# Graph network kernel: registers for sixteen steps in one load, adjacency columns fetched during the build, and two small edits around them

## The chip, the cores and the metric

The kernel runs on 1 core of one Trainium2 chip. The metric is the device time in microseconds (us) from launch to end, as the median of several executions. Engines: TensorE (PE; its weight loads are PEld, its sequencer PEq or PEldq), VectorE (DVE), ScalarE (ACT), GpSimd (POOL) and SyncE (SP), which here only issues DMAs.

## What is computed

Four graph layers over 3125 nodes with 128 features and 53125 directed edges (self loops included, sorted by destination), each added to x. The change lies in what comes before and in the first of them:

```python
h = jnp.maximum(_layernorm(x, axis=-1), 0.0)
x = x + _L0_gnn_ref(h, L0_gnn_W, L0_gnn_b, L0_gnn_gamma, L0_gnn_beta, edge_index)
# _L0_gnn_ref(x, W, b, gamma, beta, edge_index):
xw = x @ W
deg = jax.ops.segment_sum(ones, dst, num_segments=N)          # dst with N further self loops
dinv = jnp.where(deg > 0, jax.lax.rsqrt(deg), 0.0)
msg = xw[src] * (dinv[src] * dinv[dst])[:, None]
h = jax.ops.segment_sum(msg, dst, num_segments=N) + b
h = (h - mean) * jax.lax.rsqrt(var + BN_EPS) * gamma + beta   # mean, var over the nodes
h = x + jax.nn.relu(h)
```

Three more layers follow (a graph convolution with attention, a gated network of five rounds, an attention layer). They read the same edge counts and are not touched.

## The kernel before

All layers work on a dense matrix of edge counts, `adj`, 128 x 196 windows x 400 half-precision numbers in the chip's main memory. A window is 16 destination nodes; in it stand the counts of all sources. It is built once.

**The build** (`adjacency_counts`, span 37 to 335 us). The sorted edges are cut into 416 tiles of 128, and a tile that crosses a window's border is used again for the next, which gives `BSTEPS` = 611 steps. In each step DVE makes a one-hot `hot` of 400 columns (line 886; a ring of `HRING` = 8), every eighth step a one-hot `low` for eight steps (line 876), and PE adds `low`ᵀ `hot` to the PSUM bank of the step's window (line 958). Which bank that is, and how many banks must have been freed before, is data: both stand in `route_r`, two integers a step, and PE's sequencer loads them into registers:

```python
if j % 4 == 0:
    e.load(regs, route[0:1, 2 * j:2 * j + 8])
```

In the profile this is a TENSOR_LOAD of line 923, and the preparation of the eight values is one FUSED_REGOPS of line 924. A window is full after about three steps. Then ACT copies its bank to `stage` (line 975), which is a ring of `SRING` = 8, clears the bank of the window before (line 978), and SP stores the stage to `adj` (line 987). `WR` = 4 banks take turns. ACT reads the step at which each window is full from `until_r`, in loads of `WL` = 4 registers (line 970). DVE may be 8 steps ahead of PE, since a slot of the ring is free when the matmul that read it is done (`made`).

**Other work in the same loop**, at steps given by tables: node degrees on DVE (`degree_at`, steps 100 to 320, lines 842 and 846), twenty products of weights for a later layer (`fold_at`, every 12th step from 40 to 268, PE at line 938, DVE copies at line 900), and the first layer's own xw scaled by dinv, `own`, in seven groups of up to four node tiles (`hw_at`, every 16th step from 342, lines 952, 954, 909, 912). GpSimd gathers `near`, normalizes x to `h` (lines 813, 816) and casts each group of `own` to `parts[:, :, 0, :]` (line 827). The loop ends with the stores' landing and a barrier of all engines.

**The first layer** (`gcn_first`, from 335 us). The product own x adj goes by 8 chunks of destination columns (1, 3, 3, 3, 3, 4, 4 and 4 tiles of 128). SP loads a chunk to `cols` (two buffers, line 1025), DVE adds the nodes' own edges on the diagonal (`add_own`, line 1051, one operation a tile) and widens the half-precision counts to `stream` in five pieces (`widen`, line 1061), and PE multiplies (line 1138, 50 matmuls a chunk; each tile of `own` in two parts, the rounded one and the rest, which DVE makes at line 1073, `far`). Ahead of the third chunk's load stand on SP's queue eleven small loads of vectors and of the next layer's weights. PE's product for chunk 0 cannot begin before the chunk has landed, its own edges are in and a piece is widened.

## Time and profile before

| | |
|---|---|
| runs | 3403.79 us median of 3 (3402.35 to 3407.19) |
| profiled execution, its own time | 3405.62 us |
| profiled execution, span from first to last instruction | 3403.8 us, granted clock 0.861 |
| build loop | 37 to 335 us of the span |
| product of the first layer on PE | 340.3 to 421.2 us |
| busy over the whole span | PE 82%, weight loads 63%, DVE 52%, ACT 40%, POOL 28% |

The busy shares are means over stages with different limits, and the change touches only the span from 37 to about 421 us. So the rows further down are all from there, but for one from a later stage that has the same kind of instruction.

### The profile page before, as it was taken

Reading aid. Unit: us, or ns where it says so; the run is one execution under the profiler, and the core shown is the slowest. Engines: PE = TensorE matmul, PEld = TensorE weight load, DVE = VectorE, ACT = ScalarE, POOL = GpSimd, SP = SyncE. Lnnn points to the kernel's source line nnn. Section 1 sums busy time; section 2 is a strip of 40 time slices with the busy share of each in tenths; the row PEclk is TensorE's granted clock in tenths of the full one; section 3 lists DMA queues with packets and bytes.
Section 4 is the critical chain, followed back from the end, with each engine's and each line's share of the span. In section 5 each row is a group of like instructions: output and inputs, shape, how many; then the busy total and the mean of one; then the engine's idle time right before and its main releaser. Section 6 shows DMA issues by size and latency. Waiting matters only on the chain. (4 is left out here: it accounts for less than half of the span.)

```text
span 3403.8 us, 41036 instructions
## 1 busy us (share of the span) xinstructions
PE 2807.8 (82%) x13998; PEld 2155.1 (63%) x13998; DVE 1760.0 (52%) x4016; ACT 1368.7 (40%) x2596; POOL 961.7 (28%) x779
## 2 busy tenths in 40 slices
PE   5776977899998699999999999999844445446998
PEld 3333875577776578787877787877533334445775
DVE  7987765999977452111122112111534543356994
ACT  3565034699997221111111112111323333342896
POOL 6100043000000453232322231321177777750000
PEclk9977979899999799999999999999855555555999
DMA  4232633101100432121212121310242221113100
GB/s 135 100 101 88 263 130 155 39 40 40 44 1 1 192 150 97 58 92 68 87 63 90 65 92 57 116 70 1 74 141 47 46 46 38 29 21 126 78 35 20
DMA packets 79695, 266.66 MB, mean 78 GB/s; under 512 B 21129, under 2 KB 53344, under 8 KB 70176
## 3 DMA queue, kind: packets, MB, share of 16 engines
q1 hardware_dynamic: 62520, 236.50, 18.6%
q0 software_dynamic: 16976, 27.54, 3.7%
q8 instruction: 121, 1.98, 0.2%
q14 instruction: 78, 0.64, 0.1%
HBM read 232.80 MB, written 31.18 MB: 78 GB/s over the span
## 5 line engine op out<-in xcount | busy, mean ns | idle before, releaser
L2799 PE MATMUL psum<-gate_stream,parts 128*128 128x384 f32 (+1 forms) x3600 | 667.9, 344 | 16.9 <-POOL gate_stream L2872 12.5
L2799 PEld LDWEIGHTS psum<-gate_stream,parts 128*128 128x128 f32 x3600 | 631.5, 189 | 33.8 <-issue 14.4
L2872 POOL CAST gate_stream<-gate_adj 128x1920 fp32r<-128x1920 f16 (+1 forms) x200 | 371.1, 1863 | 851.3 <-PE psum L2799 828.2
L2153 PE MATMUL psum<-gat_h,gat_pair 128*128 128x129 f32 (+1 forms) x3750 | 571.1, 291 | 8.6 <-DVE gat_pair L1957 7.7
L2153 PEld LDWEIGHTS psum<-gat_h,gat_pair 128*128 128x128 f32 (+1 forms) x3750 | 461.5, 191 | 123.4 <-issue 77.7
L1485 POOL DMA_INDIRECT edge_rows<-edge_table,src_idx x440 | 431.7, 981 | 180.7 <-issue 133.7
L2890 DVE SCALAR_TENSOR_TENSOR gate_work<-psum,bhh,gate_work 128x384 f32<-128x384 f32 (+1 forms) x80 | 50.0, 626 | 793.7 <-PE psum L2762 763.1
L1957 DVE SCALAR_TENSOR_TENSOR gat_pair<-gat_above,gat_adj 128x512 f32<-128x512 f32 (+3 forms) x525 | 326.6, 622 | 86.8 <-PE psum L2153 56.7
L2066 ACT ACTIVATE gat_above<-psum,gat_as 128x512 f32<-128x512 f32 (+3 forms) x525 | 329.7, 628 | 41.4 <-PE psum L2141 39.9
L2057 ACT ACTIVATE psum<-gat_ad_rows,gat_as 128x512 f32<-128x512 f32 (+3 forms) x525 | 334.9, 638 | 16.9
L1912 DVE SCALAR_TENSOR_TENSOR gat_acc<-gat_adj,gat_q,gat_acc 128x512 f32<-128x512 f16 (+3 forms) x497 | 328.4, 677 | 0.0
L2816 ACT COPY x<-psum 128x384 f32<-128x384 f32 (+1 forms) x72 | 31.9, 488 | 545.5 <-PE psum L2799 545.5
L1722 PE MATMUL psum<-edge_rows,edge_hot 128*128 128x81 f32 x826 | 179.6, 419 | 86.0 <-DVE edge_rows L1621 86.0
L1722 PEld LDWEIGHTS psum<-edge_rows,edge_hot 128*128 128x128 f32 x826 | 177.2, 332 | 87.6 <-issue 87.2
L958 PE MATMUL psum<-count_hot,count_low 128*128 128x400 f16 x611 | 172.9, 412 | 69.8 <-DVE count_hot L886 47.2
L2141 PE MATMUL psum<-gat_r_rows,gat_pick 6*128 6x512 bf16 (+7 forms) x525 | 189.1, 361 | 0.9 <-ACT gat_r_rows L2075 0.9
L958 PEld LDWEIGHTS psum<-count_hot,count_low 128*128 128x128 f16 x611 | 88.6, 146 | 155.1 <-issue 122.3
L886 DVE TENSOR_SCALAR count_hot<-iota_hot,keyt 128x400 f16<-128x400 f16 x611 | 175.5, 339 | 16.3 <-PE psum L958 13.3
L2844 ACT ACTIVATE gate_work<-psum,brz 128x384 f32<-128x384 f32 (+1 forms) x80 | 47.1, 588 | 331.7 <-PE psum L2775 331.7
L2383 POOL MEMSET parts<- 128x512 f32 x1 | 0.5, 526 | 547.3 <-POOLq L2283 547.3
L975 ACT CAST count_stage<-psum 128x400 f16<-128x400 f32 x196 | 96.8, 494 | 126.2 <-PE psum L958 124.6
L1649 ACT ACTIVATE edge_hot<-iota,edge_minus 128x128 f32<-128x128 f32 x413 | 121.3, 391 | 6.2 <-PEq L2458 6.2
(486 smaller groups left out, 3700.8 us busy)
## 6 DMA issues: line engine op xcount, KB each, us to landing
gate_adj<-adj SPq DMA_DIRECT2D x35, 2400.0 KB, 8.1
gat_adj<-adj SPq DMA_DIRECT2D x8, 3200.0 KB, 11.3
adj<-count_stage SPq DMA_DIRECT2D x196, 100.0 KB, 1.6
gcn_adj<-adj SPq DMA_DIRECT2D x8, 2400.0 KB, 8.2
edge_place<-row_scratch SPq DMA_DIRECT2D x40, 352.0 KB, 3.8
gate_adj<-adj SPq DMA_DIRECT2D x5, 2800.0 KB, 9.1
gcn_adj<-adj SPq DMA_DIRECT2D x4, 3200.0 KB, 10.0
edge_rows<-edge_table,src_idx POOLq DMA_INDIRECT x440
```

What stands on the lines that cost most here:

```text
L886: e.tensor_scalar(hot[:, j % HRING, :], iota_hot[:], keyt[:, j:j + 1], None, ALU.is_equal).then_inc(hots, 1)
L958: e.matmul(flat[:, bass.ds(at[j % 4], ROW)], low[:, j // LS % LRING, :, j % LS], hot[:, j % HRING, :], start=False, stop=False, skip_group ...
L1485: e.indirect_dma_start(out=rows[:, c % 2, s, 0:ROWS], out_offset=None, in_=table, in_offset=bass.IndirectOffsetOnAxis(ap=self.src_idx[:, k ...
L1722: mm = e.matmul(flat[:, bass.ds(to[k % 4], SUMS)], hot_of(c)[:, s, :], rows[:, c % 2, s, :], start=False, stop=False, skip_group_check=True)
L1912: e.scalar_tensor_tensor(on, of, q[:, hi, h:h + 1], on, ALU.min, ALU.max).then_inc(most, 1)
L1957: e.scalar_tensor_tensor(on(pair, g % 2), on(above, g % 3), 1e30, cols[:, u % ring, 0:width(u) // W, hi * W:(hi + 1) * W], ALU.min, ALU.mu ...
L2057: e.activation(ps[:, 4 + g % 3, 0:up - lo], ad_rows[:, h, lo:up], ACT.Relu, bias=as8[:, hi, h:h + 1], scale=1.0 - NEG).then_inc(relus, 1)
L2066: e.activation(above[:, g % 3, 0:width(u)], ps[:, 4 + g % 3, 0:width(u)], ACT.Exp, bias=as2[:, hi, h:h + 1]).then_inc(exps, 1)
L2141: e.matmul(ps[:, 4 + g % 3, 0:width(u)], pick[:, h, :], r2_rows[:, u % 2, 0:width(u)], start=False, stop=False, skip_group_check=True).the ...
L2153: mm = e.matmul(ps[0:p, b, a:a + D + 1], pair[:, g % 2, i * P:i * P + p], h1[:, hi, h, :], start=hi == 0 and i % 3 == 0, stop=hi == NT - 1 ...
L2799: mm = e.matmul(ps[:, f, 0:hi - lo], parts[:, t, m, f, :], stream[:, (NGG * i + t // GG) % GR, 0:windows(i), t % GG * W:(t % GG + 1) * W], ...
L2872: e.tensor_copy(stream[:, n % GR, 0:windows(i), :], cols[:, i % 2, 0:windows(i), g * GW:(g + 1) * GW]).then_inc(widened, 1)
```

## The change

Five edits:

1. PE's registers are loaded for `RL` = 16 steps at once (32 registers) in place of 4 steps (8 registers): 39 loads in place of 153. `route_r` and `lowt` are padded to a multiple of 16.
2. ACT's registers are loaded for 14 windows at once in place of 4: 14 loads in place of 49.
3. The columns of chunks 0 and 1 are loaded inside the build, when windows 16 and 40 have been stored (SP waits there for the stores of the windows that the chunk reads), and not behind the barrier.
4. The own edges of these two chunks are added by DVE in the last four steps of the build (`own_at`), each behind a wait for the load. `ident_h` is made at the build's start.
5. The second part of `own` (`far`) is made by GpSimd inside the build, right behind its cast.

To make room for `cols` in the build, several temporaries of the stage before and of the build now lie in tiles that are used only later (`wl` in `own`, `near` in `parts`, `hot_f`, `key_f`, `low_f` and `low_i` in `folded`, `node_row` in `h`, `later` in `norms`); their instructions are the same.

```diff
-WL = 4
+WL = 14
+RL = 16
...
-        wl = self.sb("wl", [P, LAYERS, 2, S2], F32, st)
+        wl = own[:, 0:4 * LAYERS, :].rearrange("p (l j a) w -> p l j (a w)", l=LAYERS, j=2)
...
-                    e.tensor_copy(parts[:, at, 0, :], own[:, at, :])
+                    e.tensor_copy(parts[:, at, 0, :], own[:, at, :]).then_inc(rounded, 1)
+                    e.wait_ge(rounded, n // 2 + 1)
+                    e.tensor_tensor(parts[:, at, 1, :], own[:, at, :], parts[:, at, 0, :], ALU.subtract)
...
+        own_at = {BSTEPS - 1: (0, 0), BSTEPS - 2: (1, 0), BSTEPS - 3: (1, 1), BSTEPS - 4: (1, 2)}
...
+                    if j in own_at:
+                        c, i = own_at[j]
+                        t, p = tiles[c][i]
+                        e.wait_ge(loaded[c], 16)
+                        on = cols[:, c, 8 * i:8 * i + p // W, t * W:(t + 1) * W]
+                        e.tensor_tensor(on, on, ident_h[:, 0:p].rearrange("p (w n) -> p w n", n=W), ALU.add)
...
-                regs = [e.alloc_register(self.name("route_reg")) for _ in range(8)]
+                regs = [e.alloc_register(self.name("route_reg")) for _ in range(2 * RL)]
...
-                    if j % 4 == 0:
-                        e.load(regs, route[0:1, 2 * j:2 * j + 8])
+                    if j % RL == 0:
+                        e.load(regs, route[0:1, 2 * j:2 * (j + RL)])
...
-                    e.wait_ge(freed, need[j % 4])
+                    e.wait_ge(freed, need[j % RL])
...
+                    for c, (lo, hi) in enumerate(spans[:2]):
+                        if w == hi // W + SRING:
+                            for s in range(SRING):
+                                e.wait_ge(stored[s], 16 * (hi // W // SRING))
+                            e.dma_start(cols[:, c, 0:(hi - lo) // W, :], self.adj[:, lo // W:hi // W, :]).then_inc(loaded[c], 16)
...
-                e.tensor_copy(ident_h[:], self.ident[:]).then_inc(seen, 1)
-                for n in range(NT // grp):
-                    at = slice(n * grp, (n + 1) * grp)
-                    e.tensor_tensor(parts[:, at, 1, :], own[:, at, :], parts[:, at, 0, :], ALU.subtract).then_inc(far, 1)
-                    if n == 0:
-                        e.wait_ge(seen, 1)
-                        add_own(0)
-                        for g in range(GS):
-                            widen(0, g)
-                widen(0, GS)
-                add_own(1)
+                for g in range(NGG):
+                    widen(0, g)
```

PE, the build's step 48, before: the load of registers (line 923), its preparation, a product of the folds (line 938), then the step itself; the ISA row of line 958 carries the step's wait.

```order
L923 TENSOR_LOAD route_r
L924 ISA
L938 MATMUL psum<-wih,wl 128x384 x2
L958 ISA
L958 MATMUL psum<-count_hot,count_low 128x400
```

The same place of the changed kernel, where one load in four is left:

```order
L935 TENSOR_LOAD route_r
L936 ISA x2
L937 ISA x2
L950 MATMUL psum<-wih,own 128x384 x2
L970 ISA
L970 MATMUL psum<-count_hot,count_low 128x400
```

The load stands there once in 16 steps and not once in 4, it fills 32 registers, and four instructions prepare them in place of one. The other rows are the same (`own` is now where `wl` lies).

DVE, from the last step of the build to the first pieces of chunk 1, before:

```order
L886 TENSOR_SCALAR count_hot<-iota_hot,keyt 128x400 [waits counts_made] x6
L805 UNCONDITIONAL_BRANCH
L1044 UNCONDITIONAL_BRANCH [waits barrier_Pool_Activation_PE_DVE_SP_release]
L1070 CAST gcn_ident<-ident 128x128
L1073 TENSOR_TENSOR gcn_parts<-own,gcn_parts 128x5x128
L1051 TENSOR_TENSOR gcn_adj<-gcn_adj,gcn_ident 128x8x16 [waits first_loaded0,first_seen]
L1061 CAST gcn_stream<-gcn_adj 128x640 [waits first_own_in]
L1061 CAST gcn_stream<-gcn_adj 128x640 x3
L1073 TENSOR_TENSOR gcn_parts<-own,gcn_parts 128x5x128 x4
L1061 CAST gcn_stream<-gcn_adj 128x640 [waits first_streamed]
L1051 TENSOR_TENSOR gcn_adj<-gcn_adj,gcn_ident 128x8x16 [waits first_loaded1]
L1051 TENSOR_TENSOR gcn_adj<-gcn_adj,gcn_ident 128x8x16 x2
```

The same stretch of the changed kernel, whose widening is line 1075:

```order
L905 TENSOR_TENSOR gcn_adj<-gcn_adj,gcn_ident 128x8x16 [waits first_loaded1]
L892 TENSOR_SCALAR count_hot<-iota_hot,keyt 128x400 [waits counts_made]
L905 TENSOR_TENSOR gcn_adj<-gcn_adj,gcn_ident 128x8x16 [waits first_loaded0]
L808 UNCONDITIONAL_BRANCH
L1058 UNCONDITIONAL_BRANCH [waits barrier_Pool_Activation_PE_DVE_SP_release]
L1075 CAST gcn_stream<-gcn_adj 128x640 x4
L1075 CAST gcn_stream<-gcn_adj 128x640 [waits first_streamed]
L1086 TENSOR_TENSOR x<-x,h_23 128x3200
L1075 CAST gcn_stream<-gcn_adj 128x1920 [waits first_streamed] x4
```

The wait for a load moved from behind the barrier to ahead of it, four additions of own edges with it, and the five subtractions are gone from DVE.

SP, the stores of the build and what comes between them in the changed kernel:

```order
L999 DMA adj<-count_stage 128x400 [waits counts_evicted] x17
L1004 DMA gcn_adj<-adj 128x3200 [waits counts_stored4,counts_stored5,counts_stored3,counts_stored6,counts_stored2,counts_stored7,counts_stored1,counts_stored0]
L999 DMA adj<-count_stage 128x400 [waits counts_evicted] x24
L1004 DMA gcn_adj<-adj 128x9600 [waits counts_stored4,counts_stored5,counts_stored3,counts_stored6,counts_stored2,counts_stored7,counts_stored1,counts_stored0]
L999 DMA adj<-count_stage 128x400 [waits counts_evicted] x155
```

Before, the 196 stores stood in one row there, and both loads came first behind the barrier.

## Rows read from the trace of the kernel before

**Rows 1.** Windows: length, then busy us (count) of PE, PEld, DVE, ACT, POOL; clock, DMA.

```profile
84.00:150.00 66.00, 45.63 (x159) 24.50 (x158) 64.16 (x155) 32.85 (x76) 12.04 (x6) 0.90 0.27 96
150.00:332.00 182.00, 132.77 (x495) 71.36 (x494) 143.98 (x474) 110.14 (x251) 6.47 (x11) 0.84 0.27 90
```

**Rows 2.** PE's weight loads in time: start, us, engine, operation, idle before.

```profile
49.28 0.81 PEld L958 LDWEIGHTS psum<-count_hot,count_low 128*128 128x128 f16 x4 [0.94 <-issue]
...
326.07 0.85 PEld L958 LDWEIGHTS psum<-count_hot,count_low 128*128 128x128 f16 x4 [0.89 <-issue]
```

**Rows 3.** Register loads and their preparation, by line: ns min/median/max, first and last start.

```profile
L923 PEldq TENSOR_LOAD <-route_r x153: 587/592/1162, 37.0 to 328.6; - x153
L924 PEldq FUSED_REGOPS  x153: 80/150/158, 37.8 to 329.3; - x153
L1720 PEldq TENSOR_LOAD <-edge_out_r x117: 328/333/338, 2574.0 to 3074.3; - x117
L970 ACTq TENSOR_LOAD <-until_r x49: 304/308/576, 37.0 to 325.9; - x49
```

**Rows 4.** Matmuls of the build in order of time, around a fold.

```profile
54.81 1.55 PE L958 MATMUL psum<-count_hot,count_low 128*128 128x400 f16 x4 [0.45 <-ACT psum L978]
56.35 2.92 PE L938 MATMUL psum<-wih,wl 128*128 128x384 f32 x4
59.06 3.21 PE L958 MATMUL psum<-count_hot,count_low 128*128 128x400 f16 x12
```

**Rows 5.** Groups of the build, 37 to 332 us: PE's folds, DVE's one-hots.

```profile
L938 PE MATMUL psum<-wih,wl 128*128 128x384 f32 x80 | 34.5, 558 | 10.2 <-issue 10.2
...
L886 DVE TENSOR_SCALAR count_hot<-iota_hot,keyt 128x400 f16<-128x400 f16 x611 | 175.5, 339 | 16.3 <-PE psum L958 13.3
L876 DVE TENSOR_TENSOR count_low<-iota_low,lowt 128x1024 f16<-128x1024 f16 x77 | 52.9, 686 | 27.3 <-PE psum L958 26.9
```

**Rows 6.** ACT and DVE in order of time, where DVE does not wait.

```profile
46.42 0.49 ACT L975 CAST count_stage<-psum 128x400 f16<-128x400 f32 x1 [0.78 <-PE psum L958]
46.81 0.50 ACT L978 CAST psum<-count_none 128x400 f32<-128x400 f16 x1
...
292.40 0.68 DVE L876 TENSOR_TENSOR count_low<-iota_low,lowt 128x1024 f16<-128x1024 f16 x1
293.00 1.01 DVE L886 TENSOR_SCALAR count_hot<-iota_hot,keyt 128x400 f16<-128x400 f16 x4
```

**Rows 7.** Operations of GpSimd in the build, and DVE's one-hots beside them.

```profile
86.01 8.42 POOL L816 TENSOR_SCALAR h<-h 128x3200 f32<-128x3200 f32 x1
...
218.36 0.64 POOL L827 CAST gcn_parts<-own 128x512 fp32r<-128x512 f32 x1 [10.78 <-DVE own L912]
...
L886 DVE TENSOR_SCALAR count_hot<-iota_hot,keyt x611: 302/318/8357, 37.4 to 327.3; 128x400 f16<-128x400 f16 x153
```

**Rows 8.** The first layer's start on DVE and SP, in order of time.

```profile
335.03 0.80 SPq L1025 DMA_DIRECT2D gcn_adj<-adj  x2
...
339.39 0.23 DVE L1051 TENSOR_TENSOR gcn_adj<-gcn_adj,gcn_ident 128x128 f16<-128x128 f16 x1 [3.36 <-DMA gcn_adj<-adj]
339.65 1.70 DVE L1061 CAST gcn_stream<-gcn_adj 128x640 fp32r<-128x640 f16 x4
...
342.65 0.48 SPq L2231 DMA_DIRECT2D gat_bias<-L_gnn_gat_b  x1
...
344.72 47.86 SPq L1025 DMA_DIRECT2D gcn_adj<-adj  x6
...
345.46 3.49 DVE L1081 TENSOR_TENSOR x<-x,h 128x3200 f32<-128x3200 f32 x1
...
359.00 0.50 DVE L1051 TENSOR_TENSOR gcn_adj<-gcn_adj,gcn_ident 128x128 f16<-128x128 f16 x3 [3.47 <-DMA gcn_adj<-adj]
```

**Rows 9.** PE alone in order of time, 340 to 425 us.

```profile
340.29 80.90 PE L1138 MATMUL psum<-gcn_stream,gcn_parts 128*128 128x128 f32 x400 [9.26 <-DVE gcn_stream L1061]
```

**Rows 10.** Window of PE's product for chunk 0.

```profile
340.00:345.00 5.00, 4.71 (x22) 4.74 (x23) 4.69 (x9) 0.00 (x0) 0.00 (x0) 0.50 0.91 370
```

More of the change, by code:

```diff
@@ L66 @@
 LS = 8
-LP = -(-BSTEPS // LS) * LS
+RL = 16
+LP = -(-BSTEPS // RL) * RL
 LRING = 3
@@ L536, in edge_places, with adjacency @@
         self.rows_last = far("rows_last", [8, STEPS])
-    def adjacency(self, h, own, parts, norms):
+    def adjacency(self, h, own, parts, norms, cols, ident_h, loaded):
         nc = self.nc
@@ L750, in _ @@
                     for g in range(2):
-                        mm = e.matmul(ps[:, 7, t:t + 1], later[:, g, t * P:(t + 1) * P], one_bf[0:ER, :], start=g == 0, stop=g == 1)
+                        mm = e.matmul(ps[:, 7, t:t + 1], later[0:ER, g, t * P:(t + 1) * P], one_bf[0:ER, :], start=g == 0, stop=g == 1)
                 mm.then_inc(tiled, 1)
@@ L792, in adjacency_counts @@
         by_feature = self.sb("first_t", [P, 4 * P], F32, st)
-        shaped, hw_made, hw_taken, norm_kept, norm_in = (nc.alloc_semaphore("first_" + n) for n in (
-            "shaped", "made", "taken", "norm_kept", "norm_in"))
+        shaped, hw_made, hw_taken, rounded, norm_kept, norm_in = (nc.alloc_semaphore("first_" + n) for n in (
+            "shaped", "made", "taken", "rounded", "norm_kept", "norm_in"))
         group = lambda n: range(n // 2 * 4, min(NT, n // 2 * 4 + 4))
@@ L956, in _ @@
                     e.wait_ge(hots, j + 1)
-                    e.wait_ge(freed, need[j % 4])
-                    e.matmul(flat[:, bass.ds(at[j % 4], ROW)], low[:, j // LS % LRING, :, j % LS], hot[:, j % HRING, :],
+                    e.wait_ge(freed, need[j % RL])
+                    e.matmul(flat[:, bass.ds(at[j % RL], ROW)], low[:, j // LS % LRING, :, j % LS], hot[:, j % HRING, :],
                              start=False, stop=False, skip_group_check=True).then_inc(made, 1)
@@ L995, in gcn_spans, with gcn_first @@
         return spans, [[(t, min(P, hi - t * P)) for t in range(lo // P, -(-hi // P))] for lo, hi in spans]
-    def gcn_first(self, own, parts, norms, x1, stats, load, cols, stream, ahead):
+    def gcn_first(self, own, parts, norms, x1, stats, load, cols, stream, ident_h, loaded, ahead):
         nc = self.nc
@@ L1132, in _ @@
                     for t in range(NT):
-                        if c == 0 and t % grp == 0:
-                            e.wait_ge(far, t // grp + 1)
                         if t % GG == 0:
@@ L2218, in gcn_layers @@
         norms = self.sb("norms", [P, NP], F32, first)
-        self.adjacency(h, own, parts, norms)
+        ident_h = self.sb("gcn_ident", [P, P], F16, first)
         cols = self.far("gcn_adj", [P, 2, GC // W, ROW], F16, inner)
+        loaded = [self.nc.alloc_semaphore(f"first_loaded{s}") for s in range(2)]
+        self.adjacency(h, own, parts, norms, cols, ident_h, loaded)
         stream = self.far("gcn_stream", [P, GS, GC // W, GW], F32R, inner)
@@ L2232, in load @@
             return 8
-        self.gcn_first(own, parts, norms, h, stats, load, cols, stream, ahead)
+        self.gcn_first(own, parts, norms, h, stats, load, cols, stream, ident_h, loaded, ahead)
         first.close()
```

57 lines of the change are left out of this document (28 added, 29 removed).

## Prediction

> **What bounds the kernel now.** I read the windows of the build first, then the waits of its engines, then the weight loads, the register loads and the start of the first layer. DVE is nearly full only in one stretch, 84 to 150 us: 64.16 of 66 us [rows 1]. These are the steps 100 to 220 (counted by their register loads), where the degrees run on DVE and one operation of GpSimd, 8.42 us long, holds a one-hot up for 8.36 us [rows 7]. From 150 to 332 us DVE is busy for 144 of 182. No compute engine fills that stretch; PE's sequencer does. Its weight loads come four at a time: 0.81 us of loads, then 0.94 us without any, put down to "issue" [rows 2], so a period of 1.75 us for 4 steps. In the gap stands the load of eight registers, 592 ns, and its preparation, 150 ns [rows 3]; 0.2 us are left for dispatch and the first wait. At the low clock (1.2 GHz at 326 us) the period is 0.85 + 0.89, the same [rows 2], though four matmuls then take 1.55 us [rows 4]. The clock does not set the pace, the sequencer does. "PE waits for DVE count_hot" or "for ACT psum" on a matmul row [rows 4] is mostly this load, since the engine named was done long before. DVE's own idle time, all for PE, is 16.3 + 27.3 = 43.6 us [rows 5].
>
> Behind the build, SP's first load behind the barrier is issued at 335.03, the columns let DVE go on at 339.39 after 3.36 us of waiting [rows 8], and PE starts at 340.29 and then does not stop for 80.9 us [rows 9]. Any us by which it starts earlier is gained if nothing starves it later.
>
> **Edit 1, registers for 16 steps.** The trace has loads of two sizes on this sequencer: 4 registers 333 ns (line 1720), 8 registers 592 ns (line 923) [rows 3]. That is 65 ns a register and 74 ns fixed. By this line, 32 registers take 2.15 us. Preparation is four instructions of 8 values at 150 ns, 0.6 us, and the 0.2 us of dispatch, with three instructions more, I estimate at 0.38. The gap becomes about 3.1 us. Sixteen steps without it take 15 pitches of (0.81 − 0.14)/3 = 0.22 us and a last load of 0.14, 3.5 us. Period for 16 steps: 6.6 us in place of 4 × 1.75 = 7.0. Over 611/16 = 38.2 groups: **−15 us**, if the sequencer paced everything before and after. What goes off:
> - Steps 100 to 220 were paced by DVE, so their fifth brings nothing: +3.
> - One idle stretch of 3.1 us in place of four short ones. DVE can fill its ring of 8 in it (8 × 0.23 + 0.60, about 2.5 us [rows 6]), then waits; sixteen steps of its own take 4.9 us, so at the bare steps it keeps up. Where it has copies or subtractions too, it falls short. A fold takes PE's array for 34.5/20 = 1.7 us [rows 5]. Before, the sequencer ran on meanwhile: the loads went under it, and twelve matmuls then followed without a stop [rows 4]. With 16 steps in one row the fold is hidden only if it does not stand right behind the load, as every fourth does (step 48 and every 48th after). There all ring slots are full and the steps wait for the array: some 1.3 us each, five of them, two in the stretch already left out: +4. Below, this could be nothing; above, 20 × 1.7 = 34 us, if no fold hid at all, but the loads still follow two in three of them closely.
> - The clock: more rest and denser bursts may grant 1.2 GHz more often. Sixteen matmuls then take 16 × 1.55/4 = 6.2 us at most, under the 6.6 us of the sequencer, so I take 0.
>
> Sum for edit 1: **−8 us**.
>
> **Edit 2, ACT's registers.** Loads of 4 take 308 ns [rows 3]; at 65 ns a register, 14 take 0.96 us. ACT stops for about 1.3 us 14 times in place of 0.5 us 49 times. It has slack on the mean, but PE's bursts are now dense. An eviction and a clear take 0.78 us of ACT (twice 0.39 between starts) [rows 6], and a window takes PE 3.1 × 0.22 = 0.68 us in a burst. With four banks PE can go about six steps, 1.4 us, ahead of an open eviction. So a stop of 1.3 us costs from 0 to 0.6 us: 14 × 0.15 = **+2**, between 0 and +8.
>
> **Edit 5, subtraction on GpSimd.** No row has GpSimd with two inputs of 128x512. A cast of that size takes 0.64 us, the clear of 128x3200 8.42 us, so 1.35 for 512 [rows 7]; I take the larger, since two inputs are read. The clear held a one-hot for all of its length, so I count a full stop of DVE: seven times 1.35 us, most of it covered where DVE is up to 8 steps ahead: **+2**, from 0 to 7 × 1.35 = 9. If it took longer than 8 steps of cover, PE would wait for count_hot.
>
> **Edit 3, early columns.** SP's waits for windows 0 to 7 and 0 to 31, behind stores 16 and 40, are for stores long landed. Behind SP's wait stand only further stores. The 2.4 MB move in about 9 us among stores whose ring holds 8 windows, some 12 us at 295/196 = 1.5 us a window: 0, at worst 3 us once. **0**
>
> **Edits 3 to 5 behind the barrier.** DVE's first operation there becomes the widening of chunk 0, at 335.1 in place of 339.65 [rows 8], so PE starts at about 335.7 instead of 340.3: **−4.6**. Is it kept? Chunk 0 takes PE 10.7 us (50 matmuls at the low clock's 4.71/22 = 0.214 [rows 10]), to 346.4. DVE widens five pieces to 337.4, adds x for 3.49 us [rows 8] to 340.9, and has chunk 1 ready. The third chunk's load was issued at 344.72 and arrived at 359.00, 14.3 us later, behind 3.2 MB and eleven small loads [rows 8]. Now the small ones go first, from 335.03 (they ended at 343.1 behind 0.8 us of the two big ones [rows 8]), and it is issued at about 342.4 with no big load ahead: there by 353, and needed when chunk 1's 50 matmuls are done, at about 356. Four own-edge additions of 0.22 us in the build's last steps lie under the last register load: 0. If the landing stayed at 14.3 us, it would come at 356.7 and PE would lose about 2 of the 4.6.
>
> **Sum.** Build −8 + 2 + 2 = −4, behind it −4.6: −8.6 (−9 rounded). The profiled execution took 3405.62 us with a span of 3403.8, so 3396.6 for its like; it lies 1.8 above the median of 3403.79, so the forecast is **3395 us**.
>
> **Rivals.**
> A, the forecast: linear loads, small losses of the bursts. Own range 3386 to 3402, chance 0.50.
> B, the load's time is mostly fixed: then 32 registers take about as long as 8. DVE becomes the bound, and of its 43.6 us of idle time [rows 5] nearly all goes: 3404 − 44 − 5 = 3355. Against it are the 333 and 592 ns, which grow with the number [rows 3]. Chance 0.10. The Trainium skill, "DMA: Bandwidth & Descriptors", section "Latency and other measured facts", gives tensor_load a floor of about 600 ns that unrolling amortizes; read as a cost that stays, it leads to this same time, and a load of 333 ns in this trace lies below such a floor.
> C, the bursts eat edit 1: period of 16 steps stays at 7.0 through folds, ring and ACT; only the 4.6 remain: 3399. The stretch already bound by DVE speaks for it. Chance 0.25.
> D, slower: ACT paces the bursts. A burst of 16 steps closes 5.1 windows, 5.1 × 0.78 = 4.0 us instead of 3.5, and if ACT's long stops cannot be hidden, 14 × 1.3 = 18 us more. Build: +38 × 0.5 + 18 − 8 = +29, with the 4.6 about 3428. It decides as soon as PE waits for a cleared bank more than some 0.9 us a burst in all. Against it: four banks, and ACT idle for 105 of the 248 us of the two windows [rows 1]. A partial case lies at 3412. Chance 0.15.
>
> **Numbers.** A measurement of this kernel tells about 0.2%, 7 us, from no change: 3397 to 3410.6 is the same. Faster: 0.38 of A, all of B, 0.07 of C, 0.55. The same: 0.12 of A, 0.17 of C, 0.03 of D, 0.32. Slower: 0.12 of D and 0.01 of C, 0.13. The range is 3376 to 3411: it leaves out B and most of D, 0.2. A alone is 3386 to 3402.
>
> **What would show it.** Line 935: 39 loads with a median near 2.15 us, two preparations each on lines 936 and 937 of 150 ns. PE's gap every 16 steps near 3.1 us. Build's end at about 331 and not 335, PE's product (line 1141 of the changed kernel) beginning some 9 us earlier, at 331 to 332, with no stop later. One-hots stretched to over 1 us seven times between 218 and 306 us. The prediction is wrong if the load of 32 registers is far from 2.15 us either way, if PE's matmuls wait for ACT's clear in the middle of a burst, or if the build loses more than 4 us to the folds in steps 40 to 268.

## The result: slower by 0.94%

| | before | after |
|---|---|---|
| median, us | 3403.79 (3402.35 to 3407.19) | 3437.51 (3430.25 to 3441.9) |
| ratio | | 1.0094, interval 1.0079 to 1.011 |
| profiled execution, us (its span) | 3405.62 (3403.8) | 3430.25 (3428.6) |
| PE's sequencer, first register load to the last matmul of the build, us | 37.0 to 330.5 | 36.6 to 370.6 |

The forecast was 3395 us, in 3376 to 3411. The kernel is 34 us slower. PE's first product behind the build starts 34.2 us later than in the trace of before, so the whole loss has happened by then; of what follows, some us are given back in the stage of gathers of the profiled execution (32.3 us late at 2377 us of the trace of before, 24.8 at its end).

The same instructions as in [rows 3], in the changed kernel. Columns: engine queue, operation, count, shortest/median/longest ns, first and last start.

```profile
L935 PEldq TENSOR_LOAD <-route_r x39: 2127/2381/2802, 36.6 to 367.3; - x39
...
L936 PEldq FUSED_REGOPS  x77: 80/180/188, 39.0 to 369.7; - x77
...
L937 PEldq FUSED_REGOPS  x77: 42/80/175, 39.5 to 369.9; - x77
...
L982 ACTq TENSOR_LOAD <-until_r x14: 1223/2316/3579, 36.6 to 351.4; - x14
```

PE's load is close to the predicted 2.15 us. ACT's load, predicted at 0.96, has a median of 2.32. Starts and durations alternate: windows 0, 28, 56, ... take 1.2 to 1.5 us and windows 14, 42, ... 3.1 to 3.6.

What PE waits for in the whole build, before and after (line waited for: us in total, times, longest):

```profile
PE psum L958 <- DVE count_hot L886: 47.2, 70, 7.0
PE psum L958 <- ACT psum L978: 20.5, 28, 0.9
PE psum L938 <- issue: 10.2, 19, 0.7
...
PE psum L958 <- issue: 1.6, 4, 0.5
```

```profile
PE psum L970 <- issue: 48.6, 19, 3.5
PE psum L970 <- DVE count_hot L892: 36.6, 18, 5.6
PE psum L950 <- issue: 14.8, 5, 3.1
PE psum L970 <- ACT psum L990: 13.2, 7, 3.3
```

and what DVE waits for after, in the build and then in the steps 112 to 224. There it waited for PE 2.7 us in all before (1.4 and 1.3) and was busy for 52 of 54.6 us.

```profile
DVE count_hot L892 <- PE psum L970: 70.9, 46, 4.4
DVE count_low L881 <- PE psum L970: 4.6, 6, 2.1
```
```profile
DVE count_hot L892 <- PE psum L970: 10.1, 8, 2.1
DVE count_low L881 <- PE psum L970: 3.3, 4, 2.1
```

DVE waited for PE 40.2 us before (13.3 + 26.9 [rows 5]) and 75.5 now, and PE does not stand less for it: 79.5 us before and 113.2 now. Each of the two stands while the other works. The windows of the steps 224 to 608, before and after (length, busy us of PE, PEld, DVE, ACT, POOL, granted clock, DMA share, GB/s):

```profile
153.00:330.00 177.00, 129.23 (x484) 69.59 (x482) 142.06 (x465) 108.26 (x247) 6.47 (x11) 0.84 0.27 90
```
```profile
172.00:370.00 198.00, 126.39 (x480) 76.47 (x479) 146.12 (x463) 105.91 (x247) 14.94 (x18) 0.79 0.25 81
```

The same work takes 21 us longer. PE's weight loads are busy for 6.9 us more, DVE for 4.1 and GpSimd for 8.5 (the subtractions), which does not make 21, and the granted clock is lower.

What a burst costs shows in PE's weight loads around one group of 16 steps (columns as in [rows 2]):

```profile
198.30 0.85 PEld L970 LDWEIGHTS psum<-count_hot,count_low 128*128 128x128 f16 x4 [3.56 <-issue]
199.32 0.17 PEld L970 LDWEIGHTS psum<-count_hot,count_low 128*128 128x128 f16 x1 [0.17 <-issue]
...
201.65 0.70 PEld L970 LDWEIGHTS psum<-count_hot,count_low 128*128 128x128 f16 x4 [0.17 <-issue]
202.69 0.14 PEld L970 LDWEIGHTS psum<-count_hot,count_low 128*128 128x128 f16 x1 [0.33 <-issue]
206.39 0.85 PEld L970 LDWEIGHTS psum<-count_hot,count_low 128*128 128x128 f16 x4 [3.57 <-issue]
```

Four steps go at a pitch of 0.23 us, then seven at 0.33 (six rows are left out). The granted clock of 199.3 to 201.6 us is 0.50, that is 1.2 GHz, and 0.33 us is the pitch of the matmuls there. The gap for the load is 3.56 us instead of 3.1, the period 8.1 instead of 6.6. Behind the build, the barrier is as predicted:

```profile
370.62 0.94 ACT L987 CAST count_stage<-psum 128x400 f16<-128x400 f32 x2 [2.59 <-PE psum L970]
...
373.90 1.70 DVE L1075 CAST gcn_stream<-gcn_adj 128x640 fp32r<-128x640 f16 x4 [5.91 <-PEq L808]
...
374.45 5.81 PE L1141 MATMUL psum<-gcn_stream,gcn_parts 128*128 128x128 f32 x26 [3.42 <-DVE gcn_stream L1075]
```

PE follows DVE's first widening at 0.55 us, where before SP's load at 335.03 stood 5.3 us ahead of PE's start at 340.29 [rows 8, 9]. From the end of the build's last matmul to the product it is 3.4 us and was 9.3. That is why a build 40.5 us longer brings the product only 34.2 us later.

### The profile page after: what moved, and what is told of

Read it like the earlier page. It is cut to its first block and busy times, and to the rows that moved or that the text cites. A ratio compares the mean times of both kernels' runs of the same rounds, so it can differ in the third digit from the quotient of the medians.

```text
span 3428.6 us, 40875 instructions
## 1 busy us (share of the span) xinstructions
PE 2806.3 (82%) x13998; PEld 2160.9 (63%) x13998; DVE 1762.4 (51%) x4011; ACT 1366.1 (40%) x2596; POOL 963.5 (28%) x786
## 5 line engine op out<-in xcount | busy, mean ns | idle before, releaser
L2804 PE MATMUL psum<-gate_stream,parts 128*128 128x384 f32 (+1 forms) x3600 | 667.2, 344 | 15.5 <-POOL gate_stream L2877 11.1
L2804 PEld LDWEIGHTS psum<-gate_stream,parts 128*128 128x128 f32 x3600 | 630.8, 188 | 32.4 <-issue 12.9
L2877 POOL CAST gate_stream<-gate_adj 128x1920 fp32r<-128x1920 f16 (+1 forms) x200 | 370.6, 1861 | 849.9 <-PE psum L2804 828.2
L2060 ACT ACTIVATE psum<-gat_ad_rows,gat_as 128x512 f32<-128x512 f32 (+3 forms) x525 | 334.9, 638 | 16.9
```

The source lines that it names most:

```text
L2060: e.activation(ps[:, 4 + g % 3, 0:up - lo], ad_rows[:, h, lo:up], ACT.Relu, bias=as8[:, hi, h:h + 1], scale=1.0 - NEG).then_inc(relus, 1)
L2804: mm = e.matmul(ps[:, f, 0:hi - lo], parts[:, t, m, f, :], stream[:, (NGG * i + t // GG) % GR, 0:windows(i), t % GG * W:(t % GG + 1) * W], ...
L2877: e.tensor_copy(stream[:, n % GR, 0:windows(i), :], cols[:, i % 2, 0:windows(i), g * GW:(g + 1) * GW]).then_inc(widened, 1)
```

## The experiments

The kernels of a group ran on one chip beside runs of the kernel before, so each has its own comparison (the third and the fourth group on the same chip). The first group's chip is like the one of the traces above (before: 3406.6 us there). On the chips of the other groups the kernel before takes 3713 to 3746 us; where is shown last. There whole times say little about the build, and the stretches of the build are compared instead, between records of the wait ahead of each step's matmul on PE's sequencer.

### First group: the edits apart

e1, edit 1 alone:

```diff
-LP = -(-BSTEPS // LS) * LS
+RL = 16
+LP = -(-BSTEPS // RL) * RL
...
-                    if j % 4 == 0:
-                        e.load(regs, route[0:1, 2 * j:2 * j + 8])
+                    if j % RL == 0:
+                        e.load(regs, route[0:1, 2 * j:2 * (j + RL)])
```

> The kernel before with edit 1 alone (32 registers for 16 steps in one load; ACT's loads stay at 4). Theory R (the ring): the bursts of 16 steps outrun the four banks and ACT, and this alone makes most of the loss, so the build grows by 20 to 30 us and the time is 3424 to 3434. Theory L (ACT's loads of 14 registers, which take 1.4 or 3.1 to 3.6 us, make the loss): the build shrinks or stays, 3395 to 3406, and PE's long waits ahead of a step's bank are few.

Measured: 3435.35 us, ratio 1.009 (1.0069 to 1.0111), **+28.8 us**. Steps 112 to 224 take 65.7 us (before 54.6), steps 224 to 608 188.8 (176.6). Nothing of ACT's loads, the columns or GpSimd is in this kernel, so the bursts alone carry most of the loss. The time is 1.4 us over theory R's range. The build is 326.4 us long and was 293.5; of the 32.9 us, 12.2 arise in the steps 224 to 608, 11.1 in 112 to 224, 6.0 in 64 to 112 and 3.6 ahead of those. One group at the low clock, late in its build (line 959 is the step's matmul, 976 the eviction, 979 the clear):

```profile
348.64 5.58 PE L959 MATMUL psum<-count_hot,count_low 128*128 128x400 f16 x16 [3.13 <-issue]
348.99 0.86 PEld L959 LDWEIGHTS psum<-count_hot,count_low 128*128 128x128 f16 x4 [0.21 <-issue]
349.23 0.49 ACT L976 CAST count_stage<-psum 128x400 f16<-128x400 f32 x1 [2.90 <-PE psum L959]
349.23 1.35 DVE L887 TENSOR_SCALAR count_hot<-iota_hot,keyt 128x400 f16<-128x400 f16 x4 [2.37 <-PE psum L959]
...
350.97 0.50 ACT L979 CAST psum<-count_none 128x400 f32<-128x400 f16 x1
...
351.97 0.50 ACT L979 CAST psum<-count_none 128x400 f32<-128x400 f16 x1
...
353.34 0.17 PEld L959 LDWEIGHTS psum<-count_hot,count_low 128*128 128x128 f16 x1 [0.16 <-issue]
...
356.32 0.81 PEld L959 LDWEIGHTS psum<-count_hot,count_low 128*128 128x128 f16 x4 [2.82 <-issue]
```

The period is 7.7 us, and the granted clock of the burst 0.50. The sequencer's own records: it is through its waits at 351.51 and 352.51, just behind the clears that end at 351.47 and 352.47, and starts the load at 352.95, 0.4 us before the array's last weight load of the group. It cannot run further ahead, since a window's bank must have been evicted and cleared, and that follows the array's 0.33 us a step. So about 2.9 us of the load's path stand behind 5 us of array time. With 4 steps a group, four matmuls of 1.55 us lay beside a gap of 0.89 + 0.85 us of weight loads [rows 2, 4], and the clock did not show.

e2, edit 2 alone:

```diff
-WL = 4
+WL = 14
```

> The kernel before with edit 2 alone (ACT loads 14 registers; PE's loads stay at 8). Theory R: PE's short groups leave ACT slack enough, and even a stop of 3.3 us seven times costs at most 2 us each beyond the banks: 3404 to 3416, at most +12. Theory L: +30 us or more, 3434 and up. Either way seven of the fourteen loads take over 3 us if the start's distance from a multiple of 16 bytes decides.

Measured: 3415.9 us, ratio 1.0031 (1.0021 to 1.0041), **+9.3 us**, inside theory R's range. Its build is 6.3 us longer (299.8) and its product starts 7.4 us later than in the trace of before. Its loads:

```profile
L970 ACTq TENSOR_LOAD <-until_r x14: 1224/2277/4382, 37.4 to 317.9; - x14
```

e4, the changed kernel with ACT's registers in rows of 16 integers, 14 used, so that the loads start 64 bytes apart:

```diff
-        route_r, until_r = self.sb("route_r", [1, LP, 2], I32, st), self.sb("until_r", [1, NW], I32, st)
+        route_r, until_r = self.sb("route_r", [1, LP, 2], I32, st), self.sb("until_r", [1, NW // WL, 16], I32, st)
...
-                        e.load(regs, until_r[0:1, w:w + WL])
+                        e.load(regs, until_r[0:1, w // WL, 0:WL])
```

> The changed kernel with until_r laid out in rows of 16 integers, 14 used, so that every load of 14 registers starts at a multiple of 64 bytes. If the start's place decides their time, all fourteen take about 1.4 us and none 3. Theory R: the time falls by the seven long stops' excess only, 7 x 1.9 = 13 us at the most, 3424 to 3432. Theory L: it falls by over 20 us, to 3417 or lower. If the length of the load depends on something else, half of them stay over 3 us and the time stays at 3437.

Measured: 3433.21 us, ratio 1.0088 (1.0068 to 1.0108), where the changed kernel had 1.0094 (1.0079 to 1.011). By the whole time the two cannot be told apart. The trace is clearer: steps 224 to 608 take 189.8 us and not 198.4, the build 327.3 and not 334.0, and all 14 loads are short:

```profile
L982 ACTq TENSOR_LOAD <-until_r x14: 1218/1382/1481, 37.0 to 345.2; - x14
```

So a load of 14 registers took 1.4 us where it starts on a multiple of 16 bytes and some 3.3 where it starts 8 bytes off. Together with PE's bursts the long ones cost 6.7 us of the build. With short ones it is only 0.9 us longer than e1's, where ACT loads four registers at a time.

e3, edits 3 to 5 alone, from the changed kernel:

```diff
-RL = 16
+RL = 4
...
-WL = 14
+WL = 4
```

> The changed kernel with both register loads as before (4 steps, 4 windows), so edits 3 to 5 alone. Both theories: PE's first product starts 0.6 us behind the barrier and not 5.3, and the subtraction on GpSimd (1.39 us, for which a one-hot of DVE takes 1.75 in place of 0.69) is covered by PE's loads but for some 0 to 4 us: 3399 to 3403 us. If the subtraction stopped PE each time, 3406.

Measured: 3396.28 us, ratio 0.9972 (0.9959 to 0.9985), **−10.3 us**, 2.7 us below the range expected. Its product starts only 1.2 us earlier than in the trace of before: the build is 296.8 us long instead of 293.5, and that takes 3.3 of the 4.7 gained at the barrier. Its profile gains 1.8 us more from the product's start to the second layer, 2.8 from there to 1207 us and 3.5 behind it, in the stage of gathers above all. At 1207 us the three parts stand at +31.3 (e1), +9.4 (e2) and −5.8 (e3), sum +34.9, and the changed kernel at +32.4: the edits add up to within 2.5 us.

### Second group: what holds the bursts

f1 is edit 1 with a short clear; f2 is the control, the kernel before with the same short clear. ACT clears 16 of the 400 columns of a window, so the other counts are left uncleared:

```diff
-                        e.copy(ps[:, (w - 1) % WR, 0:ROW], none[:]).then_inc(freed, 1)
+                        e.copy(ps[:, (w - 1) % WR, 0:W], none[:, 0:W]).then_inc(freed, 1)
```

> Edit 1 alone, and ACT clears only 16 of the 400 columns of a bank, so each window's clear takes some 0.2 us in place of 0.5 (this part of the computation is left out: the counts keep sums of earlier windows). Theory B (banks: with 16 steps in a row PE runs into the banks that ACT has not yet freed, since a window may begin only when the third before it is evicted and the one before that cleared): the long gaps ahead of a step's bank wait, 32 us in edit 1 alone, fall to under half, and the time falls by 12 us or more from 3435. Theory H (DVE's ring of 8 one-hots limits): the time stays within 5 us of 3435.

> The control: the kernel before with the same short clear (again left out: most of the clearing). PE is held by its register loads there, so both theories say under 4 us of change, 3402 to 3408.

f3 is edit 1 with 16 one-hot slots:

```diff
-HRING = 8
+HRING = 16
...
-LRING = 3
+LRING = 4
```

> Edit 1 alone with a ring of 16 one-hots and of 4 low tiles in place of 8 and 3, so DVE can fill a whole burst during the load. Theory H: the long gaps ahead of a step's one-hot wait (26 us, 23 times) go, and the time falls from 3435 by 15 us or more. Theory B: those gaps shrink by half or less since banks stop PE instead, and the time falls by 8 us at the most.

f4 is edit 1 with two matmuls of 512 float32 columns, whose product nobody reads, ahead of each load after the first:

```diff
+                    if j % RL == 0 and j:
+                        for i in range(2):
+                            e.matmul(ps[:, 5, 0:512], self.ident[:], self.x[:, 4 * i:4 * i + 4, :], start=True, stop=True)
                     if j % RL == 0:
                         e.load(regs, route[0:1, 2 * j:2 * (j + RL)])
```

> Edit 1 alone, with two single-precision matmuls of 512 columns into an unused bank put ahead of each load but the first (about 0.9 us each at 2.4 GHz), so that TensorE works while its sequencer loads. Theory C (the clock: PE's array rests for 3 us in 7 and is granted 1.2 GHz for 41% of the build in place of 27%, and at 1.2 GHz a burst of 16 takes 5.3 us and a period 7.9 and not 7): the share at 1.2 GHz falls under 20% and the time falls by 8 to 15 us. If the clock costs nothing, the time stays or rises by up to 10 us for the filler.

Measured against before on this chip (3745.68): f1 3751.26, ratio 1.0017 (1.0005 to 1.0029); f2 3741.39, 0.9994 (0.9981 to 1.0007); f3 3740.93, 0.9985 (0.9969 to 1.0001); f4 3750.57, 1.001 (0.9997 to 1.0023). The stretches follow, with the runs of the other groups. The waits for a bank are the gaps of over 0.3 us ahead of that wait on PE's sequencer, summed over the build; the clock is that of the window row of steps 224 to 608; the build goes from the first register load to the last matmul. Its length is to be compared within one kind of chip alone: on the chips of the groups f, g and h the first 64 steps take 13 to 29 us more in every kernel.

| kernel | steps 112-224, us | steps 224-608, us | clock | bank waits, us | build, us |
|---|---|---|---|---|---|
| before | 54.6 | 176.6 | 0.84 | 3.6 (x6) | 293.5 |
| after | 66.1 | 198.4 | 0.79 | 45.9 (x52) | 334.0 |
| e1, edit 1 | 65.7 | 188.8 | 0.79 | 32.1 (x37) | 326.4 |
| e2, edit 2 | 56.5 | 181.2 | 0.84 | 8.8 (x10) | 299.8 |
| e3, edits 3 to 5 | 56.6 | 177.1 | 0.87 | 3.4 (x5) | 296.8 |
| e4, after, loads aligned | 66.1 | 189.8 | 0.81 | 34.3 (x41) | 327.3 |
| f2, before, short clear | 52.2 | 174.8 | 0.89 | 6.7 (x9) | 308.2 |
| f1, edit 1, short clear | 66.1 | 181.7 | 0.85 | 25.3 (x31) | 332.7 |
| f3, edit 1, 16 slots | 64.4 | 178.4 | 0.84 | 47.0 (x52) | 329.1 |
| f4, edit 1, filler | 61.9 | 175.5 | 1.00 | 16.9 (x22) | 320.8 |
| g1, edits 3 to 5 | 53.3 | 176.0 | 0.87 | 4.5 (x7) | 311.5 |
| g2, 8 steps a load, edits 3 to 5 | 63.7 | 177.1 | 0.89 | 13.2 (x17) | 324.9 |
| g3, edits 3 and 4 | 54.2 | 176.1 | 0.88 | 6.5 (x9) | 308.3 |
| g4, edit 1, 16 slots, filler | 57.8 | 172.6 | 1.00 | 23.7 (x23) | 309.8 |
| h1, edits 1, 3, 4, 11 slots, filler | 62.9 | 173.3 | 0.99 | 25.7 (x24) | 314.7 |
| h2, edits 3 and 4 | 53.3 | 175.9 | 0.91 | 5.2 (x8) | 309.7 |
| h3, edit 1 again | 64.3 | 191.8 | 0.79 | 29.7 (x37) | 334.6 |
| h4, edits 3 to 5 | 54.8 | 175.8 | 0.90 | 6.9 (x10) | 311.4 |

Edit 1 alone did not run on this chip. Its stretches on the two others (e1, h3) are 3 us apart or less, and they are what the aids are compared with. Each aid takes the steps 224 to 608 from 189 down to 175 to 182 us, and no aid alone gets far below before's 176.6. More slots turn waits for one-hots into waits for banks: gaps of over 0.3 us ahead of the one-hot wait add up to 25.9 us in e1, 5.7 in f3, and those for banks rise from 32.1 to 47.0. A shorter clear does the reverse (31.1 and 25.3). They are one chain: bursts pass on their stop to whichever neighbour has the smaller ring. So neither theory B nor theory H held as written. In the steps 112 to 224 neither slots nor clear helped (64.4 and 66.1 us against 65.7): with 16 slots DVE still waits for PE 13.0 us there, as much as in e1 (13.5). Only with the filler does that stretch get shorter, 61.9 us, and 57.8 with 16 slots besides. The filler acts on the clock. Around its loads the matmuls' rows, line 962 the step, 925 the filler:

```profile
343.73 3.94 PE L962 MATMUL psum<-count_hot,count_low 128*128 128x400 f16 x16 [1.46 <-issue]
347.51 1.88 PE L925 MATMUL psum<-x,ident 128*128 128x512 f32 x4
350.77 3.87 PE L962 MATMUL psum<-count_hot,count_low 128*128 128x400 f16 x16 [1.38 <-issue]
```

Period 7.0 us, where e1 has 7.7 to 7.9 at the low clock. Work that nobody reads shortens the stretch, as theory C had it. Its granted clock goes from 0.79 to 1.00 when the gaps are filled, and it is 13 us shorter than e1's and 16 than h3's. By the whole time, 4.9 us over before on this chip, no gain can be read.

### Third group: eight steps, GpSimd's subtraction, both aids

g1 is e3 once more. g2 is the changed kernel with `RL = 8` in place of 16, so 16 registers for 8 steps, and `WL = 4` in place of 14. g3 is g1 with edit 5 taken back:

```diff
-                    e.wait_ge(rounded, n // 2 + 1)
-                    e.tensor_tensor(parts[:, at, 1, :], own[:, at, :], parts[:, at, 0, :], ALU.subtract)
...
-                for g in range(NGG):
-                    widen(0, g)
+                for n in range(NGG):
+                    at = slice(n * GG, (n + 1) * GG)
+                    e.tensor_tensor(parts[:, at, 1, :], own[:, at, :], parts[:, at, 0, :], ALU.subtract)
+                    widen(0, n)
```

g4 is f3 and f4 together, measured once.

> Edits 3 to 5 alone once more, as the control of the two kernels beside it and on another chip than the first time: 7 to 11 us under the kernel before, if what the first run showed (4.7 us at the barrier, some 3 us given back in the build, the rest in later stages) holds.

> Edits 3 to 5 with registers for 8 steps in a load (16 registers). A load of 16 should take 4 groups of 4 registers, about 1.1 us (0.27 us a group of 4, from 0.33, 0.59 and 2.15 us for 4, 8 and 32). Theory S (stops of under 2 us are covered by the banks, the ring and the clock's memory): the build is 3 to 12 us shorter than with 4 steps. Theory L (any longer stop loses): it is the same or longer, by 0 to 8 us.

> Edits 3 and 4 alone: the subtractions are done by DVE behind the barrier again, each ahead of its piece of the widening, and GpSimd does only its casts. If GpSimd's subtraction costs the build 7 x 1.1 us of DVE's time that PE sees in part, the build is 1 to 4 us shorter than in the control; PE's product starts 0.8 us later behind the barrier; together -3 to +1 us against the control.

> Edit 1 alone with both aids: the ring of 16 one-hots and the filler matmuls ahead of the loads. If the clock and the ring are separate causes, steps 224 to 608 take 168 to 174 us (before 176.6, edit 1 alone 188.8, with the ring 178.4, with the filler 175.5). If they are the same waiting counted twice, they take 175 or more.

Measured against before there (3718.8): g1 3729.04, ratio 1.0033 (1.0021 to 1.0045); g2 3720.2, 1.0009 (0.9992 to 1.0025); g3 3717.4, 0.9998 (0.9985 to 1.0011); g4 3717.36, once. The load of g2, against 592 ns for 8 registers [rows 3] and 2381 for 32:

```profile
L935 PEldq TENSOR_LOAD <-route_r x77: 3/1264/3397, 37.1 to 359.6; - x77
```

The load grows linearly with its registers, some 0.3 us for each four. Even 8 steps a load give nothing (177.1 against 176.0), and lose 10 us in the steps 112 to 224, where DVE is nearly full; the build is 13.4 us longer than g1's, more than theory L allowed. Edits 3 to 5, 10.3 us faster on the first chip and expected 7 to 11 us faster here, are 10 us slower. Without edit 5 (g3) the build is 3.2 us shorter, as expected; the whole is 11.6 us shorter, which was not.

g4's 172.6 us lie in the range for separate causes, but the two aids overlap: alone they gave 10.4 and 13.3 us against e1, together 16.2 and not 23.7.

### Fourth group: edit 1 and edits 3 to 5 once more, and the parts that looked best

h1 is the changed kernel without edits 2 and 5 (`WL = 4`, and the diff of g3), with the filler of f4 and `HRING = 11`; h3 is e1, h4 is e3 and h2 is g3 once more.

> The changed kernel with its registers for 16 steps and its early columns (edits 1, 3 and 4), without edits 2 and 5, with two matmuls of 512 float32 columns ahead of each load after the first, and with as many one-hot slots as there is room for: 11 in place of 8. Theory 1 (the bursts lose to the low clock, to the ring and to the banks, and each aid gives its part back): steps 224 to 608 take 173 to 178 us (before 176.6, the changed kernel 198.4), steps 112 to 224 58 to 62 us, the share of the build at 1.2 GHz is under 0.2, PE starts the first product 0 to 5 us earlier than the kernel before does in its own run; the whole is 0 to 6 us faster than before or the same. Theory 2 (what made it slower is the load itself on PE's sequencer, whatever stands beside it): steps 224 to 608 at 185 us or more, and the whole at least 10 us slower than before.

> Edit 1 alone once more, on another chip and beside the kernels of this call. Theory 1 (the build's loss is there on every chip, what the whole time shows of it depends on the stage of gathers at the end): steps 112 to 224 take 64 to 67 us, 224 to 608 186 to 191 us, and on a chip whose last stage is as long as in the trace of before the whole is 20 to 32 us slower; on a chip with the long last stage it is anywhere from 0 to 30. Theory 2 (the loss was one of that chip): 224 to 608 near 177 us.

> Edits 3 to 5 once more, with registers as before. Theory 1 (they gain the 4.7 us behind the barrier and lose about 3 in the build; the rest of what two earlier comparisons showed, 10 us less and 10 us more, is of the last stage): the first product starts 1 to 2 us earlier than before's, the whole is within 10 us of before on either side, and a chip with the short last stage gives 3 to 11 us less. Theory 2 (the change of the tiles' places gains in the later stages): the whole is 8 to 12 us faster again, with the anchors from the second convolution on falling as in the first comparison.

> Edits 3 and 4 once more, the subtraction on DVE as before. Theory 1: the build as before (290 to 296 us on a chip without the slow first steps), 2 to 4 us shorter than with the subtraction on GpSimd; behind the barrier PE starts about 4 us later into its product than with edit 5 less the subtractions, 5 x 0.3 us, that is about 3 us earlier than before. The whole 0 to 12 us faster than before. Theory 2 (edit 5 costs nothing in the build): the two builds within 1 us.

Measured against before there (3713.45): h1 3710.61, ratio 0.9985 (0.9971 to 1.0); h3 3720.7, 1.0012 (0.9996 to 1.0028); h4 3728.77, 1.0034 (1.0023 to 1.0046); h2 3714.5, 0.9998 (0.9986 to 1.001). In h1 the steps 224 to 608 take 173.3 us and 112 to 224 62.9, the first as theory 1 had it, the second 1 us over its range. So low clock, slots and banks account for the loss in the steps 224 to 608, and the theory that the load itself costs it falls. In 112 to 224, where DVE is nearly full, 9.6 us against h2 remain. Over the whole build h1 is 5.0 us longer than h2 and 6.4 longer than g3, which is the same program as h2; its product starts 4.3 us later than h2's. g4, with 16 slots, is as long as the builds with registers for 4 steps on this chip (309.8 us against 308.3 to 311.5). So with both aids the bursts cost up to 6 us of the build, and gain nothing.

(The steps before 112 cannot be compared piece by piece. GpSimd's clear of 8.4 us, which holds up one operation of DVE for as long, falls on the steps 55 to 58 in h2, 61 to 65 in g3 and 64 to 75 in h1. So h2 and g3, one program, take 55.1 and 46.0 us for the first 64 steps and 23.3 and 30.2 for the next 48.)

h3's build is as long as e1's in the stretches that count (64.3 and 191.8), and its product starts 28.5 us later than h2's, yet its whole time is only 7 us above before and 6 above h2's. In the profiles it is 30.4 us behind h2 up to 2377 us of the trace of before, ahead of the last stage, and 1.7 us ahead of h2 at the end. Where did they go? Its gathers, line 1485 to 1488 in the kernels. First before on its own chip, then h2 (columns as for the loads):

```profile
L1485 POOL DMA_INDIRECT edge_rows<-edge_table,src_idx x440: 951/956/1993, 2470.6 to 3035.1; - x147
...
  issue: 133.7, 439
```
```profile
L1488 POOL DMA_INDIRECT edge_rows<-edge_table,src_idx x440: 949/955/2466, 2480.9 to 3319.1; - x147
...
  PE psum L1725: 278.0, 6
  issue: 132.0, 433
```

The operations are as long, but GpSimd waits six times, 278 us in all, for PE to have used the rows that it gathered before, and never in the trace of before. The 40 loads of `edge_place` in that stage stretch too, from 2480.2 to 3053.9 us in h2, from 2469.9 to 2807.4 before; what PE itself waits for there is not settled. In h3 the gathers begin at 2512.0, 31 us behind h2's, and end at 3314.8, 4 us ahead of them. So on this chip the last stage keeps a pace of its own, which varies by more than the builds differ. The kernel before was not profiled there, so its own stage of gathers is not known. h4's whole time is 15.3 us over before's, outside the 10 us of its theory 1; its build is 1.7 us longer than h2's.

## Why the prediction was wrong

**The −15 of edit 1 was there, on the sequencer's own records.** In the changed kernel the loads take 93.6 us where they took 99.6, the gaps ahead of them 3.2 where they took 12.7, and the preparation is the same: −15.5. But the gaps ahead of the waits for a bank grew from 51.3 to 93.5 us, those ahead of the waits for a one-hot from 43.5 to 58.0: +56.7. The sum, +41, is the build's growth from 293.5 to 334.0, in which edits 2 and 5 have their share.

**The failed step** is "the clock ... under the 6.6 us of the sequencer, so I take 0", and with it the −15 + 3 + 4 of edit 1. The build changed by +33 us in e1 where −8 was summed. The sum treated 16 steps as sequencer time plus the load, with the other engines running on behind four banks and eight slots. The runs showed three things in its place.
- At 1.2 GHz the array sets a burst's pace, and banks and slots let the sequencer run only a few steps ahead, so array time and load add up: 7.7 to 8.1 us and not 6.6. Even at the high clock throughout, in f4, where the filler is in it, a group took 7.0 us, no gain over 4 × 1.75 [rows 2]. I compared 6.2 us of array (16 matmuls took 5.58 in e1's group) with a period of 6.6 as if the two could lie side by side for the whole of it; they can only as far as the sequencer may run ahead. The sign named for this came: a step in the middle of e1's burst waits until ACT's clear ends at 351.47.
- With the longer rests the granted clock of the steps 224 to 608 was 0.79 and not 0.84. With filler in the gaps it was 1.00, and 13 us of 188.8 came back.
- Steps 112 to 224, paced by DVE, "bring nothing": they lost 11 us. DVE, busy for 51.5 us of them as before, now waits for PE 13.5 us in e1 where it waited 2.7. A stop of 3.1 us against 2.5 us of slots was in the text; that it is paid out of the nearly full engine was not. But 16 slots alone gave back only 1.3 us (f3), the filler 3.8 (f4) and both 7.9 (g4). So the slots are not the whole of it, and how the 11 us divide is not settled. No run takes the folds out, so the +4 for them, ten of which lie in these steps, was not tried either.

**Size of the load**: right, 2.38 us at the median against 2.15. Preparation was right in sum (about 32 us before and after).

**Edit 2**, +2 (0 to 8): +9.3 alone. The size of a load was wrong, 2.3 us at the median and not 0.96. The rule of 65 ns a register came from loads of 4 and 8 registers, every one a multiple of 16 bytes on from the one before, so [rows 3] could not show the other kind. Kept aligned it is 1.4 us, still more than the line gives, and it then costs the build about 1 us beside PE's bursts (e4 against e1).

**Edit 5**, +2 (0 to 9): right in size. An operation takes 1.39 us, predicted 1.35. What of it stops DVE shows beside the one that starts at 315.81 us in the changed kernel:

```profile
314.95 1.13 DVE L892 TENSOR_SCALAR count_hot<-iota_hot,keyt 128x400 f16<-128x400 f16 x3
316.00 1.75 DVE L881 TENSOR_TENSOR count_low<-iota_low,lowt 128x1024 f16<-128x1024 f16 x1
317.67 0.54 DVE L892 TENSOR_SCALAR count_hot<-iota_hot,keyt 128x400 f16<-128x400 f16 x2
```

The operation of 0.69 us takes 1.75, 1.06 us more, six times (the seventh subtraction is of 128x128 and takes 0.46). In the third and fourth group the build is 3.2 and 1.7 us longer with edit 5 than without, and the product starts 1.7 and 0.8 us later, since a subtraction of 0.82 us is gone from ahead of the first widening. The whole times are 11.6 and 14.3 us apart for it, on the chip with the long last stage. Up to 2377 us of the trace of before the profiles are 2.7 and 0.8 us apart, so the rest is made in the last stage; its cause stays open.

**Edits 3 and 4, behind the barrier**: right. 5.3 us from SP's load to PE's start became 0.6 from the first widening to it, the way from the build's last matmul to the product is 4.7 us shorter in e3 (predicted 4.6), and the gain was kept to the product's end (34.2 against 34.8 us late). The third chunk's load, issued at 379.00, was in time.

**Rivals.** D, slower at 3428, came nearest, with 3437.5. Its deciding point, more than 0.9 us a burst of waiting for a cleared bank, was passed in the changed kernel: 45.9/39 = 1.2 us in the long gaps alone (in e1 32.1/39 = 0.8). Its mechanism was half of it: ACT's long stops count (edit 2), but e1 without them has the larger share. Its chance of 0.15 was too low, because the argument against it counted ACT's idle time on the mean. B is excluded by the load's size. The Trainium skill, "DMA: Bandwidth & Descriptors", section "Latency and other measured facts", puts tensor_load's floor at about 600 ns. These runs disagree, with 305 to 308 ns for ACT's four registers in e1 and time that grows with the number. C's "period stays at 7.0" is what f4's groups at the high clock show. B's 43.6 us of idle time for PE were misread: the rows put 40.2 of it down to PE [rows 5].

**Open**: why the last stage is some 270 us longer on some chips (its gathers span 838 us in h2 and 565 in before's trace) and what moves it by 10 to 20 us from kernel to kernel, so also whether edits 3 to 5 are a gain in general. On the first chip they are 10.3 us faster than before; on another one, twice, they were 10 and 15 us slower, and edits 3 and 4 alone equal to before. How much of the first chip's −10.3 beyond the barrier comes from the tiles' new places was not tried apart.

## What to carry to other kernels

A stop on a sequencer is hidden only as far as the rings around it let the neighbours run. Before putting n short stops into one long one, compare its length with the ring in steps (here 8 slots and four banks, some 2 us, against 3.1). In the stretch where DVE was nearly full, it paid most (11 us in 112 steps), and a ring twice as long did not give that back. Check whether the price even has a fixed part: here 4, 8, 16 and 32 registers took 0.31, 0.59, 1.26 and 2.38 us, so 39 loads in place of 153 saved 6 us of 99.6, and 9.5 us of gaps ahead of them.

Rests in the matmul stream had a second price in the granted clock (0.79, and 1.00 with the rests filled). Of a table that is loaded into registers, keep every group at a multiple of 16 bytes: 14 registers took 1.4 us so and 3.3 otherwise. And where two chips differ by 9% of the whole time, mostly in a late stage, compare the stage that was edited by its own anchors. Such an anchor must not have a long operation of another engine fall now on one side of it and now on the other, as the clear does with step 64 here.

## What was not expected of the hardware

- A load of 14 registers took 1.2 to 1.5 us from a multiple of 16 bytes and 3.1 to 3.6 from 8 bytes beside one (up to 4.4 in e2); in e4, with all of them aligned, none took over 1.48.
- Two matmuls of 512 float32 columns in each gap raised the granted clock of the steps 224 to 608 from 0.79 to 1.00 and made them 13.3 us shorter (f4 on the second group's chip against e1 on the first's), although PE had 96 more records of work there.
- A float32 subtraction of 128x512 on GpSimd (1.39 us) stretched the DVE operation beside it from 0.69 to 1.75 us.
- The kernel before took 3404 and 3407 us on two occasions and 3713 to 3746 on others. By the kernels profiled there, most of the difference lies in the last stage and in the first 64 steps of the build (44 to 59 us there, 30.5 in before's trace), both of which run beside indirect gathers. That the gathers cause it was not tried.
